# Taking the rounding constant off on GpSimd in a blockwise FP4 feed-forward

## The reference

```
def fp4_quant_dequant(x):                 # blocks of 16 along the last dim
    scale = max(abs(xb), axis=-1) / 6.0;  scale = maximum(scale, 1e-12)
    xn = xb / scale
    idx = searchsorted(_MID, abs(xn))     # grid 0, .5, 1, 1.5, 2, 3, 4, 6
    return _GRID[idx] * sign(xn) * scale

gate = fp4_linear(x, w_gate)              # 128 -> 352, both operands quantised
y = fp4_linear(x, w_up)
h = silu(gate) * y
return fp4_linear(h, w_down)              # 352 -> 128, h quantised
```

## Time and profile before

| | |
|---|---|
| median of the timed runs | 1207.08 us |
| the profiled execution | 1213.22 us |
| its span | 1211.5 us |
| mean granted TensorE clock | 0.947 of full |
| busy over the span | PE 89%, DVE 77%, ACT 60%, POOL 39% |

### The profile page before, as it was taken

How to read it: one execution, slowest core, us unless ns; L and a number is a source line. 1 busy time by engine, 2 the same in 40 slices (tenths; PEclk the granted TensorE clock), 3 DMA queues, 4 the chain that set the end, 5 groups by cost and what they waited for, 6 DMA issues and landing times. The chain is left out here.

```text
span 1211.5 us, 22302 instructions
## 1 busy us (share of the span) xinstructions
PE 1084.0 (89%) x7591; PEld 598.0 (49%) x7598; DVE 932.6 (77%) x1978; ACT 723.7 (60%) x1110; POOL 472.1 (39%) x807
## 2 busy tenths in 40 slices
PE   4757888999999999999999687999988989999997
PEld 2435664333434333343434364444444358888874
DVE  7979997878888888888886364778778546777776
ACT  3647641566666666666666353456656667778761
POOL 7101220133323323333552320566776712566630
PEclk9979996899999999999999787799999889999999
DMA  4322592011221222122101023222222253687552
GB/s 138 100 86 70 113 143 27 19 54 55 71 65 57 89 72 72 55 84 74 44 2 35 1 79 89 60 63 65 64 63 65 68 187 126 195 247 232 163 131 79
DMA packets 99953, 106.10 MB, mean 88 GB/s; under 512 B 21505, under 2 KB 77334, under 8 KB 99776
## 3 DMA queue, kind: packets, MB, share of 16 engines
q1 hardware_dynamic: 93904, 95.65, 29.6%
q0 software_dynamic: 4992, 8.48, 2.1%
q10 hardware_dynamic: 944, 0.54, 0.2%
HBM read 65.20 MB, written 38.45 MB: 86 GB/s over the span
## 5 line engine op out<-in xcount | busy, mean ns | idle before, releaser
L1241 ACT ACTIVATE a_probs<-a_pst 128x1024 f32<-128x1024 f32 (+4 forms) x544 | 412.0, 808 | 212.9 <-PE a_pst L1185 199.7
L1264 DVE TENSOR_REDUCE a_tops<-a_ps 128x1 f32<-128x512 f32 (+9 forms) x624 | 338.1, 589 | 74.1 <-PE a_ps L1139 66.7
L1078 POOL TENSOR_SCALAR_AFFINE_SELECT a_probs<-a_probs 128x256 f32<-128x256 f32 (+3 forms) x384 | 180.3, 481 | 333.2 <-ACT a_probs L1241 328.2
L1139 PE MATMUL a_ps<-kp,qp 96*128 96x256 bf16 (+10 forms) x2112 | 293.0, 253 | 15.0 <-DVE a_tops L1264 7.5
L1185 PE MATMUL a_pst<-qp,kp 98*128 98x512 bf16 (+4 forms) x1088 | 262.4, 333 | 16.5 <-ACT a_probs L1241 11.9
L1139 PEld LDWEIGHTS a_ps<-kp,qp 96*128 96x128 bf16 (+1 forms) x2112 | 140.8, 99 | 222.0 <-DVE a_tops L1264 101.1
L1204 PE MATMUL a_po<-a_probs,vh 128*32 128x512 f32 (+4 forms) x2176 | 230.5, 500 | 7.0 <-POOL a_probs L1078 5.5
L1264 DVE TENSOR_REDUCE a_tops_lead<-a_ps 128x1 f32<-128x512 f32 x256 | 165.1, 685 | 19.4 <-PE a_ps L1139 18.7
L1185 PEld LDWEIGHTS a_pst<-qp,kp 98*128 98x128 bf16 (+1 forms) x1088 | 83.8, 100 | 113.4 <-ACT a_probs L1241 61.8
L1882 POOL DMA_INDIRECT chosen_rows<-e_slot_y,e_slot_x x92 | 93.9, 1021 | 97.1 <-DVE e_slot_y L2102 58.7
L2090 DVE TENSOR_TENSOR e_tails<-e_hidden,e_heads 128x512 fp32r<-128x512 f32 x124 | 85.8, 695 | 32.7 <-ACT e_heads L2024 28.0
(11 more groups left out here) (329 smaller groups left out, 1518.5 us busy)
## 6 DMA issues: line engine op xcount, KB each, us to landing
e_slot_w<-weight_parts SPq DMA_DIRECT2D x23, 1024.0 KB
qp<-q_parts SPq DMA_DIRECT2D x64, 96.0 KB
slot_rows<-empty_row SPq DMA_DIRECT2D x4, 1495.0 KB, 27.1
e_slot_x<-slot_rows SPq DMA_DIRECT2D x23, 260.0 KB
a_raw<-in_wraw SPq DMA_DIRECT2D x18, 256.0 KB, 4.1
weight_parts<-first_rows SPq DMA_DIRECT2D x9, 512.0 KB, 4.7
weight_parts<-a_cut SPq DMA_DIRECT2D x9, 512.0 KB, 3.0
qp<-q_parts SPq DMA_DIRECT2D x64, 64.0 KB
```

The source lines that it names most:

```text
L1078: pool.affine_select(out=seen, in_=seen, compare_op=ALU.is_ge, fill=0.0, base=m0, pattern=[[0, 2], [1, mw]], channel_multiplier=-1 if laye ...
L1139: last = pe.matmul(bank[:, i * room + at:i * room + to], sb["qp"][slot][0:rows, j, f["qt"] * P:(f["qt"] + 1) * P], sb["kp"][slot][0:rows, ...
L1241: act.activation(probs[local % RING][0:st["rows"], 2 * part:2 * part + 2, st["off"]:CHUNK], p_st[part][0:st["rows"], :, st["off"]:CHUNK], ...
L1264: dve.tensor_reduce(out, scores, AX.X, ALU.max).then_inc(s["banks_read"], 1)
```

## The change

VectorE's second step of `quantise` (L738) is gone. In its place GpSimd, ahead of the rescaling of the pair, takes `f_m` off with a subtraction of two tensors (new L616) and then MAGIC with a multiply by one and an addition (new L618), each waiting for the one before by the new semaphore `grid_left`. The subtraction writes into a buffer of `f_hq`, the addition and the rescaling work in place there, and `f_hq` has two buffers. The numbers of VectorE's semaphore (`scaled`, `rounded`) are one less per pair. The subtraction waits for the transposes of two pairs back, no longer of the pair before; VectorE's L728 (now L733) waits for the subtraction of two pairs back, no longer for its rescaling.

```diff
@@ -77,7 +77,7 @@
         heads_done rests_done middles_done tails_done v_copied
         q_stored0 q_stored1 k_stored0 k_stored1""",
     "ffn": """
-        operand_cleared gate_up_done silu_done hidden_steps magic_done hq_ready hq_turned hqt_copied down_done y_added""",
+        operand_cleared gate_up_done silu_done hidden_steps magic_done grid_left hq_ready hq_turned hqt_copied down_done y_added""",
     "attention": """
         banks_filled banks_read split_steps maxima_stored scores_t_ready
         exp_done unseen_zeroed pv_done v_staged o_copied inverse_done""",
@@ -560,7 +560,8 @@
         REST = INNER % P
         PAIRS = TILES // 2
         act_gate = tmp("f_silu", [P, 2 * INNER])
-        h, hq = (tmp(n, [P, 2 * NB, FPB]) for n in ("f_h", "f_hq"))
+        h = tmp("f_h", [P, 2 * NB, FPB])
+        hq = [tmp(f"f_hq{i}", [P, 2 * NB, FPB]) for i in range(2)]
         hv, hm = ([tmp(f"{n}{i}", [P, 2 * NB, FPB]) for i in range(2)] for n in ("f_v", "f_m"))
         am, inv = (tmp(n, [P, 2 * NB]) for n in ("f_am", "f_inv"))
         sc = [tmp(f"f_sc{i}", [P, 2 * NB]) for i in range(3)]
@@ -570,15 +571,15 @@
         p_turn = [bank(f"f_pt{i}") for i in range(2)]
         p_down = [bank(f"f_pd{i}") for i in range(2)]
         s = sb["counts"]["ffn"]
-        MULTS, SCALES, QUOTIENT, EXPONENTS, ROUNDED, QUANTISED = 2, 6, 7, 8, 1, 2
+        MULTS, SCALES, QUOTIENT, EXPONENTS, ROUNDED = 2, 6, 7, 8, 1
 
         def scaled(i, step):
 
-            return START + EXPONENTS * i + QUANTISED * max(0, i - 1) + step
+            return START + EXPONENTS * i + ROUNDED * max(0, i - 1) + step
 
         def rounded(i, step):
 
-            return START + EXPONENTS * min(i + 2, PAIRS) + QUANTISED * i + step
+            return START + EXPONENTS * min(i + 2, PAIRS) + ROUNDED * i + step
 
         flat = lambda a: a[:, :, :].rearrange("p a b -> p (a b)")
         block = ctx.enter_context(nc.Block())
@@ -608,10 +609,15 @@
         @block.gpsimd
         def _(pool):
             for i in range(PAIRS):
-                pool.wait_ge(s["hidden_steps"], rounded(i, QUANTISED))
-                if i:
-                    pool.wait_ge(s["hq_turned"], START + 2 * i)
-                fp4_rescale(pool, hv[i % 2][:, :, :], sc[i % 3][:, :], hq[:, :, :]).then_inc(s["hq_ready"], 1)
+                mine = hq[i % 2]
+                pool.wait_ge(s["hidden_steps"], rounded(i, ROUNDED))
+                if i >= 2:
+                    pool.wait_ge(s["hq_turned"], START + 2 * (i - 1))
+                pool.tensor_tensor(flat(mine), flat(hv[i % 2]), flat(hm[i % 2]), ALU.subtract).then_inc(s["grid_left"], 1)
+                pool.wait_ge(s["grid_left"], START + 2 * i + 1)
+                pool.tensor_scalar(flat(mine), flat(mine), 1.0, -MAGIC, ALU.mult, ALU.add).then_inc(s["grid_left"], 1)
+                pool.wait_ge(s["grid_left"], START + 2 * i + 2)
+                fp4_rescale(pool, mine[:, :, :], sc[i % 3][:, :], mine[:, :, :]).then_inc(s["hq_ready"], 1)
 
         @block.tensor
         def _(pe):
@@ -632,7 +638,7 @@
                     for k in range(3):
                         cols = min(P, INNER - k * P)
                         last = pe.transpose(p_turn[u][0:cols, k * P:(k + 1) * P],
-                                            flat(hq)[:, u * INNER + k * P:u * INNER + k * P + cols], sb["ident"][:, :])
+                                            flat(hq[i % 2])[:, u * INNER + k * P:u * INNER + k * P + cols], sb["ident"][:, :])
                     last.then_inc(s["hq_turned"], 1)
 
             def down(i):
@@ -722,8 +728,7 @@
                 fp4_scales(dve, h[:, :, :], am[:, :], sc[i % 3][:, :], inv[:, :], step, scaled(i, MULTS),
                            (s["hq_ready"], START + i - 2) if i >= 3 else None)
                 if i >= 2:
-                    dve.wait_ge(s["hq_ready"], START + i - 1)
-                    dve.wait_ge(step, rounded(i - 2, QUANTISED))
+                    dve.wait_ge(s["grid_left"], START + 2 * (i - 2) + 1)
                 v, m = hv[i % 2][:, :, :], hm[i % 2][:, :, :]
                 dve.tensor_tensor(v, h[:, :, :], inv[:, :].unsqueeze(2).broadcast_to(wide), ALU.mult).then_inc(step, 1)
                 dve.wait_ge(step, scaled(i, QUOTIENT))
@@ -734,8 +739,6 @@
                 v, m = flat(hv[i % 2]), flat(hm[i % 2])
                 dve.wait_ge(s["magic_done"], START + i + 1)
                 dve.scalar_tensor_tensor(v, m, MAGIC, v, ALU.add, ALU.add).then_inc(step, 1)
-                dve.wait_ge(step, rounded(i, ROUNDED))
-                dve.scalar_tensor_tensor(v, v, -MAGIC, m, ALU.add, ALU.subtract).then_inc(step, 1)
 
             for i in range(PAIRS + 1):
                 if i < PAIRS:
```

## The result

The kernel after takes 1212.10 us (median of 6 runs, 1210.65 to 1214.49), the kernel before beside it 1207.43 (6 runs, 1205.38 to 1209.98): a ratio of 1.0039, 95% interval 1.0025 to 1.0053, so 4.7 us slower (3.0 to 6.4). 1214 had been forecast, with a range of 1207 to 1220. Beside the last three experiments one execution of the kernel before took 5549 us; no ratio or interval here counts it.

A forecast was written before the change was run, and what follows sets the result against it. DVE was taken to set the feed-forward's pace at 5.90 us a pair. Blocking between DVE and GpSimd (+4.2) and the stage's end (+2.5) sum to +6.7 us on the 1207.08 median: forecast 1214, range 1207 to 1220.

The forecast's parts named there:

- The collisions of the earlier trace: Feed-forward's end and kernel's start: DVE's two-SBUF-input instructions and TENSOR_SCALARs exclude GpSimd's, whichever asks first; forecast built on this, 67%.
- GpSimd's lengths: GpSimd's added subtraction and addition per pair, 704 elements each: 1.68 and 0.79 us.
- The pair, 6.05 to 6.46, taken 6.20: Feed-forward mid-stage: a pair goes from 5.90 to 6.20 us, +4.2 us over fourteen pairs, bounds +2.1 and +7.8.
- Outcome (b): Mid-stage pair: L733 (L728 before) gets the port before the rescaling, L735 (L730 before) waits 1.07 us; pair 6.05 us.
- outcome (c): Mid-stage pair: the addition beats L133, then L138 is held behind the rescaling; +1.48, pair 6.46 us.
- outcome (a): Mid-stage pair: the rescaling is first and L733 (L728 before) waits for it, +1.26; pair 6.24 us.
- The end, +2.5: Feed-forward's end after the fifteenth L736: +1.6 us, +2.4 with TensorE at half clock, up to +4; taken +2.5.
- The waits and the second buffer at nothing: Feed-forward: new semaphore waits, TensorE's later rescaled pair and the second buffer add nothing beyond the end's sum.
- No blocking: Rival, mid-stage: no exclusion, pairs of 5.0 to 5.3 us, -8 to -13, +2.5 at the end, about 1199; 11%.
- The gain just given back: Rival, mid-stage: only about 0.9 us is lost, pairs stay at 5.9 us, only the end costs, 1209; 14%.
- The clock falling in mid-stage: Rival: TensorE's wait lowers its clock, about 1 us a pair more over 8 to 14 pairs, 1223; 8%.
- The sum, +6.7 us: Whole kernel: +4.2 mid-stage and +2.5 at the end, giving 1213.8 from the median, forecast 1214.

The follow-up runs named there:

- the last three experiments: The kernel before, the kernel after and run 7's kernel, unchanged, on one chip again: against before, after 1.0035 and run 7's 0.9926.
- run 1: The kernel before with one more GpSimd pass per pair (v - MAGIC, 704 elements) ahead of the rescaling, L738 keeping its length: ratio 1.0066, 8.0 us slower.
- run 3: The kernel after without GpSimd's addition of -MAGIC, so another output: 0.9981 of before, 2.3 us under it.
- run 6: The kernel after with f_m's rows padded (11 rows of 64, 8 unused after each): 0.9987 of before, 1.6 us under it.
- run 7: Run 5's kernel with f_inv's rows also padded (11 rows of 4, 4 unused after each): 0.9919 of before, 9.8 us under it.
- the second pair of profiles: The kernel before and the kernel after, unchanged, profiled again on one chip: the after kernel's feed-forward 4.2 us longer.
- run 2: The kernel before with the second buffer of rounded values alone: ratio 1.0002, 5.90 us a pair.
- run 5: The kernel after, but ScalarE makes the whole rounding constant and GpSimd takes it off in one subtraction: 0.9954 of before, 5.6 us under it.

## Why the prediction was right, and where its terms were off

- *The collisions of the earlier trace rows decide the case.* Right, and shown by the kernel after and runs 1, 3, 6 and 7: five different instructions of VectorE (in this order L735, L133, L138, L741, L733) were held, each the one that was to come next at the port, and each let go within 0.05 us of GpSimd's end apart from its own work behind the port.
- *GpSimd's lengths*, 1.68 and 0.79 us, taken from 512 elements and 0.17 us fixed: 1.682 and 0.792. Of the 0.792, 0.014 are a hold: the same addition takes 0.778 in run 1, where nothing is in its way, and here it starts 0.04 us behind L133.
- *The pair, 6.05 to 6.46, taken 6.20.* Outcome (b) came in thirteen of the fourteen pairs, L733 starting 1 to 10 ns ahead of the rescaling, at 6.04 in the timeline; outcome (c) came in one, 6.42 us for a forecast of 6.46; outcome (a) in none. The term was mis-sized because I took a value between (a) and (b) although both are discrete: +2.3 us over the fourteen pairs, where +4.2 had been taken and +2.1 was the bound (and +1.96 in the second pair of profiles, just under it). The prices of (b) and (c) were right; which outcome would come the prediction could not tell, and it came out at the cheapest. The price of (b) itself, L735 held by 1.07 us, was measured as 1.59 - 0.53 = 1.06.
- *The end, +2.5.* +2.73 in the first profile, with the events where they had been put: last rescaling done after 9.45 us (9.5), TensorE there after 10.3 (10.4), at half clock. In the second it is +1.61, with TensorE at full clock and waiting for the rescaling, which is the +1.6 of the same paragraph (its 14.4 is 9.5 + 4.81 = 14.3 and a hand-over). So the rescaling's end is understood, and the half clock, which makes the difference between the two, was luck. One step was wrong and cost nothing: the sixteenth L741 was to be ready 1.06 us after the fifteenth, and started 2.18 after it (182.02), for ScalarE makes its constant behind its copies of the transposed pair, and TensorE had got that pair late (the constant was begun at 181.09). The subtraction held the port until 2.64 in either case, so it ended at 3.39 (3.40).
- *The waits and the second buffer at nothing.* Right by run 2; TensorE's wait for the rescaled pair grew to 1.02 us and cost nothing, as run 6 shows, which hands the pair over as late and is shorter.
- *The rivals.* No blocking: excluded by runs 1 and 6. The gain just given back: the pair is 0.14 to 0.17 us longer than before, so it is more than given back. The clock falling in mid-stage: the granted clock of the stretch is 0.98, 0.97 before. Both have a slower part at its start (0.83 from 100 to 110 us after, 0.95 before); from 110 to 180 us it is 1.00 in the kernel after, with 1.02 us of idle time of TensorE in the pair shown.
- *The sum, +6.7 us.* +4.7. The mid-stage term came 1.9 to 2.2 us lower, the end 0.2 higher or 0.9 lower; the first pairs, -0.99 and +0.63 in the two pairs of profiles, were not in the sum.

The Trainium skill's rule in "SBUF — State Buffer", section "Who interferes with whom", that the two engines exclude each other for whole instructions, agrees with these rows but for the start: some 0.14 us at the start of a held or holding instruction lie outside, as the prediction had it (the rescaling ends 1.24 us after L733, and takes 1.39 by itself). It also says that an instruction of VectorE with at most one SBUF input outside the two-port modes does not take part. Run 6 agrees: L735 at 0.89 us runs beside the rescaling. That 0.53 us is such a mode and 0.89 is not is argued from that page; the profile shows the durations only.

## What to carry to other kernels

Before work is moved from VectorE to GpSimd, lay both engines' instructions side by side in one period and mark those that exclude each other: here 0.92 us saved on VectorE turned into 1.06 us of waiting. What mattered here was where GpSimd's instruction ends, not how long GpSimd is idle; a pass of 0.8 us into 4.5 idle us made the stage 6.7 us longer and the kernel 8.0. Where a small or one-input instruction is the one that is held, making it slower by itself with padded rows, so that it is no longer held, can be worth more than its speed.

## What the runs showed of the hardware that was not expected

A TENSOR_SCALAR of VectorE from SBUF to SBUF, 704 elements of 4 bytes, takes 0.53 us and is held by GpSimd; with the output in 11 rows of 64 with a gap of 8 it takes 0.89 us and is not held. Writing the two shapes differently without a gap changes nothing. For 44 elements the padded form costs 0.01 us (0.199 against 0.186), and it saved 0.6 us of holding in run 7 against run 5. And an engine's turn is decided by thousandths: L733 was 1 to 10 ns ahead of the rescaling in all but one pair of the kernel after (both show as 135.13), and each time the rescaling waited for it. Behind so constant a lead stands that L133 times both: the addition starts 0.02 to 0.04 us behind it and ends 0.64 us after it in each of these pairs, whether it took 0.78 or 0.81 us.
